# An attention and expert block on one core: fractions in four buffers, two pieces of GpSimd's work on ScalarE, slope tables ahead of the projections

## What is computed

```python
x = x + tanh(g_xattn) * xattn(layernorm(x), ctx, ctx, frac, ...)
x = x + tanh(g_ffn) * ffn(layernorm(x), ...)

# xattn: Q, K, V are projections with bias, in heads of 16
logits = einsum("bhqd,bhkd->bhqk", Q, K) * 16 ** -0.5
D = clip(frac[:, None, :] - frac[:, :, None], -0.2, 0.2)
bias = alpha_pos * max(D, 0) + alpha_neg * min(D, 0)      # per head
probs = softmax(gamma * logits + delta * bias)
out = (probs @ V) @ Wo.T + bo
```

## Time and profile before

| | us |
|---|---|
| median of 3 runs | 631.6 |
| the runs | 631.97, 631.6, 625.74 |
| the profiled execution, its own time | 625.72 |
| its span in the trace | 623.9 |
| busy in it: PE, PEld | 533.2, 436.4 |
| busy: DVE, ACT, POOL | 414.9, 293.9, 305.6 |
| mean granted clock of TensorE, of its full speed | 0.908 |

### The profile page before, as it was taken

The page is one execution under the profiler, slowest core; times in us unless marked ns, Lnnn a source line. Parts: engine busy times, 40 slices in busy tenths (PEclk is TensorE's granted clock), DMA queues, the critical chain, the costliest instruction groups (busy, mean ns, idle before and its releaser), DMA issues.

```text
span 623.9 us, 17263 instructions
## 1 busy us (share of the span) xinstructions
PE 533.2 (85%) x6424; PEld 436.4 (70%) x6425; DVE 414.9 (66%) x972; ACT 293.9 (47%) x690; POOL 305.6 (49%) x217
## 2 busy tenths in 40 slices
PE   3697698889697876976978999999999999999991
PEld 0464476667575665756645666899999999999990
DVE  4788446776474846689798865776666766666660
ACT  3654144554353525344873656544444444444440
POOL 5969455745557475733767872332222222222221
PEclk9999567997796968786897999999999999999997
DMA  8400012122221212152243558532222222222221
GB/s 282 158 2 6 2 39 81 40 83 61 96 84 39 82 40 81 45 151 86 82 136 114 192 178 198 186 52 50 43 41 50 50 50 50 38 47 50 43 26 17
DMA packets 37553, 49.16 MB, mean 79 GB/s; under 512 B 8066, under 2 KB 30722, under 8 KB 37380
## 3 DMA queue, kind: packets, MB, share of 16 engines
q1 hardware_dynamic: 30356, 39.18, 21.1%
q0 software_dynamic: 7152, 9.34, 8.1%
HBM read 31.79 MB, written 16.72 MB: 78 GB/s over the span
## 4 chain that ended last, share of the span: by engine, by line
DMA 31%; PE 22%; POOL 18%; DVE 15%; issue 9%; SPq 1%; ACT 1%; POOLq 1%; DVEq 0%; ACTq 0%
PE bank L1140 20%; DMA out<-xres,idu 20%; DMA W<-frac 8%; POOL W L472 4%; POOL W L482 4%; POOL W L473 3%; POOL W L474 2%; DVE xres L1115 2%; POOL W L471 2%; POOL W L460 2%; DVE hbuf L928 1%; DMA xres<-x 1%; POOL rstd L438 1%; DVE idu L1112 1%; DVE W L885 1%
## 5 line engine op out<-in xcount | busy, mean ns | idle before, releaser
L1140 PE MATMUL bank<-W,xT 128*128 (+1 forms) x1704 | 141.5, 260 | 0.4 <-DVE xT L1096 0.4
L729 ACT ACTIVATE hbuf<-bank,b1t 128x128 f32<-128x128 f32 x312 | 89.0, 369 | 111.8 <-PE bank L1140 109.0
L555 POOL DMA_INDIRECT out<-xres,idu x39 | 60.7, 1557 | 156.1 <-DVE xres L1115 147.1
L1140 PE MATMUL bank<-W 128*128 128x17 bf16 (+3 forms) x1440 | 97.6, 219 | 37.2 <-POOL W L474 19.6
L1140 PEld LDWEIGHTS bank<-W,xT 128*128 128x128 bf16 (+1 forms) x1704 | 118.1, 102 | 15.1 <-issue 2.4
L1140 PE MATMUL bank<-xres,W 128*128 128x128 bf16 (+1 forms) x1920 | 122.6, 223 | 0.2 <-issue 0.2
L1140 PEld LDWEIGHTS bank<-xres,W 128*128 (+1 forms) x1920 | 111.8, 98 | 6.7 <-issue 0.4
L1140 PEld LDWEIGHTS bank<-W 128*128 128x128 bf16 x1440 | 71.9, 104 | 59.5 <-POOL W L474 22.4
L619 ACT ACTIVATE W<-bank 128x512 bf16<-128x512 f32 x64 | 37.3, 584 | 101.5 <-PE bank L1236 101.5
L797 DVE TENSOR_REDUCE mx<-bank 128x4 f32<-128x512 f32 x64 | 41.2, 686 | 61.5 <-PE bank L1140 61.5
L482 POOL TENSOR_TENSOR W<-stage,W 128x1024 bf16<-128x1024 f32 x28 | 60.6, 2169 | 19.7 <-ACT W L611 18.7
(11 more groups left out here) (151 smaller groups left out, 698.2 us busy)
## 6 DMA issues: line engine op xcount, KB each, us to landing
stage<-wts SPq DMA_DIRECT2D x36, 512.0 KB
xres<-xs_dram SPq DMA_DIRECT2D x39, 128.0 KB, 2.1
xs_dram<-hbuf SPq DMA_DIRECT2D x7, 645.0 KB, 6.5
W<-ctxT SPq DMA_DIRECT2D x4, 512.0 KB, 6.5
xres<-x SPq DMA_DIRECT2D x4, 512.0 KB, 8.1
out<-xres SPq DMA_DIRECT2D x4, 512.0 KB, 5.1
W<-wproj SPq DMA_DIRECT2D x4, 256.0 KB, 7.2
W<-frac SPq DMA_DIRECT2D x16, 64.0 KB, 4.6
```

Source lines behind the costliest of these rows:

```text
L555: nc.gpsimd.indirect_dma_start(out, bass.IndirectOffsetOnAxis(idu[:, par, t:t + 1], axis=0), ysb[par][t], None, compute_op=ALU.add).then_i ...
L729: ins = nc.scalar.activation(hbuf[:, q, c * TR:(c + 1) * TR], bank[UPS * par + q][:, c * TR:(c + 1) * TR], ACT.Gelu, bias=b1t[:, par, UC * ...
L1140: return nc.tensor.matmul(o, a, b, start=start, stop=stop, **kw)
```

## The change

1. The fractions have four buffers (`fr`, now in the tail of `hsplit`) instead of two. `load_frac(b + 2)` stands where `load_frac(b)` stood, and waits for `d_clipped` of four batches earlier; the first four are loaded ahead.
2. `difference(b)` is split: `clip(b)` (difference and clip) and `split_difference(b)` (the rest) stay on GpSimd; the pass that keeps the top rows becomes `top_part(b)` on ScalarE. `dx` and `dtop` exist once, so `clip(b)` waits for `split_difference(b - 1)`.
3. `norm4` moves to ScalarE as an activation with scale `rstd1` and bias `nmr`; GpSimd keeps the inverse deviation and makes `nmr` from it (`deviation4`, two more passes over 128x4).
4. `slopes` moves from VectorE's last group to a place ahead of the first, before `weight_low(3, 3)`.
5. In group 0 TensorE turns the inputs behind the values instead of ahead of them; `row` is loaded ahead of the first inputs, the first two fractions ahead of `proj(3)` and the last inputs.

The core of the diff:

```diff
-        fr = [under(T) for _ in range(2)]
+        tails = hsplit[:].rearrange("p a b n -> p (a b n)")[:, 2 * DC * T4:2 * DC * T4 + 8 * T].bitcast(fp32)
+        fr = [tails[:, k * T:(k + 1) * T] for k in range(4)]
...
             def load_frac(b):
-                if b >= 2:
-                    sp.wait_ge(d_ready, b - 1)
-                sp.dma_start(fr[b % 2], ...).then_inc(ld_fr[b % 2], 16)
+                if b >= 4:
+                    sp.wait_ge(d_clipped, b - 3)
+                sp.dma_start(fr[b % 4], ...).then_inc(ld_fr[b % 4], 16)
...
             for b in range(2, B):
-                load_frac(b)
+                if b + 2 < B:
+                    load_frac(b + 2)
                 load_piece(b // 2, b % 2)
...
-            def norm4(g):
+            def deviation4(g):
                 pool.wait_ge(ln1_stat, 4 * (g + 1))
                 link(inverse_deviation(rstd1, mv1, 4 * g, 4 * g + 4))
...
+                link(nc.gpsimd.tensor_tensor(nmr[:, 4 * g:4 * g + 4], mv1[:, 4 * g:4 * g + 4, 0], rstd1[:, 4 * g:4 * g + 4], ALU.mult))
+                nc.gpsimd.tensor_scalar(nmr[:, 4 * g:4 * g + 4], nmr[:, 4 * g:4 * g + 4], -1.0, None, ALU.mult).then_inc(ln1_rstd, 1)
...
+            def clip(b):
+                pool.wait_ge(ld_fr[b % 4], 16 * (b // 4 + 1))
...
+                if b >= 1:
+                    pool.wait_ge(d_ready, b)
+                link(nc.gpsimd.tensor_tensor(dx.rearrange("p (k t) -> p k t", k=4), fk, fq, ALU.subtract))
+                nc.gpsimd.tensor_scalar(dx, dx, ..., ALU.max, ALU.min).then_inc(d_clipped, 1)
+
+            def split_difference(b):
+                pool.wait_ge(d_top, b + 1)
                 if b >= 2:
                     pool.wait_ge(s_ps, R * (b - 1))
...
-                link(nc.gpsimd.tensor_scalar(dtop, dx, cst[:, C_LOW:C_LOW + 1], None, ALU.mult))
                 nc.gpsimd.tensor_tensor(dblk[b % 2], dx, dtop, ALU.subtract).then_inc(d_ready, 1)
...
             for b in range(B):
+                if b + 1 < B:
+                    split_difference(b + 1)
                 if b + 2 < B:
-                    difference(b + 2)
+                    clip(b + 2)
                 if b < B - 1:
                     piece_low(b // 2, b % 2)
...
+            def norm4(g):
+                act.wait_ge(ln1_rstd, g + 1)
+                if g:
+                    act.wait_ge(xT_ps, DC * g)
+                for s in range(4):
+                    b = 4 * g + s
+                    ins = nc.scalar.activation(xh[:, s * D:(s + 1) * D], xres[:, b * D:(b + 1) * D], ACT.Identity,
+                                               scale=rstd1[:, b:b + 1], bias=nmr[:, b:b + 1])
+                ins.then_inc(xh_ready, 1)
+
+            def top_part(b):
+                act.wait_ge(d_clipped, b + 1)
+                if b:
+                    act.wait_ge(d_ready, b)
+                nc.scalar.activation(dtop, dx, ACT.Copy, scale=cst[:, C_LOW:C_LOW + 1]).then_inc(d_top, 1)
...
                     context_high(g + 2)
+                if g + 1 < Q4:
+                    norm4(g + 1)
+                else:
+                    top_part(0)
                 for o in range(DC):
                     queries_high(g, o)
...
                 if u % 2 == 0:
+                    if b + 1 < B:
+                        top_part(b + 1)
                     piece_high(b // 2, b % 2)
...
             weight_low(0, 2)
+            slopes()
             weight_low(3, 3)
...
-                else:
-                    slopes()
...
-                turn_inputs(g)
+                if g:
+                    turn_inputs(g)
                 project_values(g)
+                if g == 0:
+                    turn_inputs(g)
                 project_queries(g)
```

More of the change, by code:

```diff
@@ L231, in build @@
         ld_ct = [sem(f"ld_ct{k}") for k in range(2)]
-        ld_fr = [sem(f"ld_fr{k}") for k in range(2)]
+        ld_fr = [sem(f"ld_fr{k}") for k in range(4)]
         ld_brow, brow_zero = sem("ld_brow"), sem("brow_zero")
@@ L354, in _ @@
             load_proj(1)
+            sp.dma_start(row[:], rows.to_broadcast([P, V_N])).then_inc(ld_row, 16)
             load_x(0)
-            sp.dma_start(row[:], rows.to_broadcast([P, V_N])).then_inc(ld_row, 16)
             load_proj(2)
@@ L484, in _ @@
             context_low(0)
-            norm4(0)
+            deviation4(0)
             pool.wait_ge(ld_cst, 16)
@@ L490, in _ @@
             context_low(1)
-            norm4(1)
+            deviation4(1)
             for k in range(2):
@@ L496, in _ @@
                                   ).then_inc(table_ready, 1)
+            pool.wait_ge(ld_col, 16)
             context_low(2)
-            norm4(2)
+            deviation4(2)
+            clip(0)
             context_low(3)
-            norm4(3)
-            pool.wait_ge(ld_col, 16)
-            difference(0)
-            difference(1)
+            deviation4(3)
+            split_difference(0)
+            clip(1)
             pool.wait_ge(setup_act, 2)
@@ L637, in _ @@
             weight_high(0)
+            norm4(0)
             weight_high(3)
```

57 lines of the change are left out of this document (25 added, 32 removed).

## The result

The changed kernel takes 660.27 us (median of 4 runs, 656.28 to 662.37), the kernel before 628.87 us (4 runs, 625.74 to 631.97): a ratio of 1.049, with a 95% interval of 1.041 to 1.058. It is slower, as forecast, and 9 us above the forecast's 651. The profiled execution is the slowest of the four, 662.37 us; on another occasion (last experiment) the same kernel had a median of 651.25 us.

The account below looks back on a forecast made before the run. In attention, TensorE stalls waiting for GpSimd's last pass, and the half clock behind them, were taken as the bound. 625.7 + 22 (attention) + 1.5 (projections) = 649 us, median put at 651; range 628 to 666, chance 0.58.

Parts of the forecast that it names:

- The wait for fractions: Attention, GpSimd's first pass waiting for its load (66.2 us in 12 waits before): claimed to vanish, remaining wait costed at nothing.
- The new wait: Attention: TensorE waits for GpSimd's last pass, behind ScalarE's top_part, in 15 batches; 1.92 us lost each, 1.74 idle.
- The collision: Attention: GpSimd's piece delays VectorE's short L802, by a margin under 0.1 us; full-clock batch 13.6 us instead of 11.7.
- The clock: Attention: TensorE's granted clock falls to 0.50 for about 6.8 us behind stalls in most batches; such a batch takes 14.6 us.
- 12 x 14.6 + 3 x 13.6: Attention loop: 12 batches with the clock fallen, 3 with it held; 216 us against 194.2, so +22 us.
- One stalled batch as the price: Attention: one measured batch of 14.53 us, less 0.2 for the gap, plus 0.3 for the piece, priced the likeliest batch.
- how many stalls there are counts for more than how long they are: Attention: claimed because a TensorE stall of about 1.9 us costs about 4.7 us, mostly through the clock.
- Rival 1: Attention: the clock holds and GpSimd's piece collides with VectorE, 15 batches of 13.6 us; 637 us, chance 0.12.
- The projections: Stretch before attention: loop +4.2, slope tables' new place +2.3, then -1.3 and -3.3; sum +1.9, counted as +1.5 us.
- inputs_low(0) to end 2.3 us later: Projections, group 0: slope tables at their new place on VectorE delay it by 2.3 us, bounds 0 and 6.7.
- The rest: Everything outside attention and projections: claimed to keep its time, with loads ahead of proj(3) costing some tenths.

Follow-up runs that it names:

- last experiment: The changed kernel timed once more with nothing edited: 651.25 us, ratio 1.039 to the kernel before.

## Why the prediction was right, and where it was off

- **The wait for fractions costs nothing any more.** Right: it is in no list of waits.
- **The new wait.** Right in place, count and size: 15 waits, 24.8 us (forecast about 15 waits of 1.7 us each, some 25 us), bias matmuls at +2.90 (forecast +2.93), the pass 0.70 us (taken as 0.72). The run with the pass moved shows it as the cause, not only as a neighbour.
- **The collision.** Right, though the margin was less than 0.1 us by the sum: the full-clock batch is 13.51 us (forecast 13.6), and 12.02 with the piece out of the way (forecast 11.7; the 0.3 more are VectorE's pair, 0.68 us beside GpSimd's clip instead of 0.34).
- **The clock.** The sum of the loop was +22 us; it is +24.2 and +26.6 in two executions. The term that was mis-sized is "12 x 14.6 + 3 x 13.6". In its place the runs showed other kinds of batches: in the first trace nine of 13.5 to 13.9, four of 17.0 to 17.2, and two of 14.4 and 15.0 at the ends. Only two of 15 lie between 14 and 15 us, in either trace, where the forecast had most; that its sum comes out so near is in part luck. In four of the nine short batches the mean granted clock is 0.88, and they last only 0.2 us longer than one at the full clock: TensorE then came later to the same wait, and waited less (0.65 us for L833 instead of 1.79). In the long ones the clock cost 3.7 us (17.23 - 13.51); their half-clock stretch was not 6.7 us as in the earlier trace rows, from which the price of 14.6 came, but 13.6 us long (last of the windows above). The clock's share comes out at 16 to 18 us, where the forecast's own terms held 216 - 204 = 12.
- **One stalled batch as the price.** The 14.53 us came from one of the five batches in which TensorE waited for L474 in the kernel before. The other four lasted 17.2 to 18.3 us, and two of their waits were these:

```profile
166.37 1.89 PE L1140 MATMUL bank<-W 128*128 128x128 bf16 x16 [4.75 <-POOL W L474]
...
221.47 1.89 PE L1140 MATMUL bank<-W 128*128 128x128 bf16 x16 [4.81 <-POOL W L474]
```

Their waits were 3.6 to 4.8 us of the 7.4 to 8.5 us by which these batches exceed 9.78, about half. So "how many stalls there are counts for more than how long they are" is too strong: it was read from the shortest of the five. (The price of L473, 1.15 us by the prediction, is 1.57 in the trace; the sum does not use it.)
- **Rival 1**, the clock holds and the piece collides, was priced at 637 us. The run with both gaps filled is that case made on purpose, and took 637.39.
- **The projections.** Forecast +1.5 us to the start of the scores, measured +5.6, and +3.9 to u = 1. The loop was right within 0.4 us (12.36, forecast 12.7), and so was `norm4` (2.07 us, forecast 2.0). That its place on ScalarE costs time is shown by the run that puts it behind the queries (two steps of 11.38 us); but two kernels with `norm4` on GpSimd also took 12.4 us a step on average, so that the 11.3 of the one trace of before is no firm base. Mis-sized was "inputs_low(0) to end 2.3 us later": it was 6.9 later, and 5.3 or more in all seven traces with these projections. The slope tables held VectorE from 16.74 to 24.3 us, since two instructions on 128x16 took 2.38 us beside GpSimd's fills and 1.99 beside its `context_low`, and the inputs' statistics started at 10.86 instead of 8.64. Yet in the kernel with only four buffers, whose projections run in the order of before, the scores start at 67.4 and not at 65.0: about 2.5 of the 5.6 us are not shown to come from the new order. Whether the two more loads ahead or chance made them was not tried.
- **The rest.** Forecast unchanged, and 352.3 in the second execution against 352.0. The first one's +6.2 us are of that execution. The first runs' median of 660 lies 9 us above the forecast, the second set's is 651.25, and why the two sets differ by 9 us is open: only one execution of each has a trace.

## What to carry to other kernels

When a pass is handed to another engine, its place in that engine's queue is worth more than its length: look for where that engine idles, and count what it stands behind. Then look at what the freed engine does next, for its work moves as well, and can end up in front of a short instruction of a third engine that the critical path needs. Give an idle gap on TensorE two prices, its length and the half clock behind it, and have a run that fills the gap with dead matmuls tell the second from the first.

## What the runs showed of the hardware

- **The length of an idle gap of TensorE does not decide alone whether the clock falls.** With one gap of 1.78 us in each batch of 13.5 us the granted clock stayed at 1.00 for 117 us, and then fell twice. With one of 1.72 us in each batch of 12.0 us it fell in six batches of 15, and with one of 1.79 us in each batch of about 16.8 us it fell in every one. One gap of 0.87 us in each batch never let it fall from 90 to 240 us. What decides was not tried. The Trainium skill, page "TensorE: Matmul & The Clock Gate", section "Why this matters for your kernels", asks only that there be no longer idle gaps than these; that is too mild for most of these runs, and the 117 us of the first agree with it.
- **VectorE beside GpSimd.** A 128x8 instruction of VectorE alone takes 0.17 us, and up to 2.05 us beside a GpSimd pass that reads two tensors; it then ends when that pass does. Beside GpSimd's clip, which reads one, it takes 0.47 to 0.54 us. The Trainium skill, page "SBUF — State Buffer", section "Who interferes with whom", says that a VectorE instruction with two inputs in SBUF contends with a GpSimd one that reads SBUF, and, of VectorE's two-port modes, that who issues first gets the shared ports for its whole instruction. The rows beside passes with two tensors agree (L833 with two inputs, 2.00 us; L804 with one, 2.04 us, though no run shows in which mode it runs). Those beside the clip agree only in part, as a pass of 2.07 us costs L833 only 0.3 us there.
